# Clearing 896 unused words on GpSimd ahead of every four gathers of the second graph layer

## The reference, cut to what matters

```python
h = (x @ W).reshape(n, NHEAD, OUT_FEATS)            # 6250 nodes, 4 heads of 64
h_l, h_r = (a_l * h).sum(-1), (a_r * h).sum(-1)
e = h_l[row] + h_r[col]                              # 100000 edges
e = jnp.where(e > 0, e, ALPHA * e)
ex = jnp.exp(e - segment_max(e, row)[row])
denom = jax.ops.segment_sum(ex, row, num_segments=n)
att = ex / (denom[row] + 1e-16)
out = jax.ops.segment_sum(att[:, :, None] * h[col], row, num_segments=n)
```

## Time and profile before

| | us |
|---|---|
| three runs | 4160.5, 4170.12, 4170.46 |
| median | 4170.12 |
| profiled execution, its own time | 4167.99 |
| its span | 4166.3 |
| the block of the visits, POOL's first gather to DVE's last addition | 2048.7 to 3420.0 |

### The profile page before, as it was taken

How to read it: one execution, slowest core, us unless ns; L and a number is a source line. 1 busy time by engine, 2 the same in 40 slices (tenths; PEclk the granted TensorE clock), 3 DMA queues, 4 the chain that set the end, 5 groups by cost and what they waited for, 6 DMA issues and landing times. The chain is left out here.

```text
span 4166.3 us, 48622 instructions
## 1 busy us (share of the span) xinstructions
PE 2771.2 (67%) x12850; PEld 2189.0 (53%) x12850; DVE 2489.0 (60%) x5847; ACT 1566.9 (38%) x5077; POOL 2220.9 (53%) x2162
## 2 busy tenths in 40 slices
PE   5466776567677754824666676666667665699983
PEld 4233344355555543713555465555555545599972
DVE  5345998677777786434545555555555567544438
ACT  6663000067787831113422232233233223333334
POOL 0366777766666602555256666666666641265530
PEclk9678888788898965967867767677776675799985
DMA  5232333323333313632234444444444464122234
GB/s 146 86 88 83 89 87 89 88 85 90 90 93 91 95 57 91 152 76 71 78 89 114 109 114 113 109 115 109 113 113 112 111 112 150 62 72 70 71 96 143
DMA packets 220767, 408.50 MB, mean 98 GB/s; under 512 B 51598, under 2 KB 134545, under 8 KB 220371
## 3 DMA queue, kind: packets, MB, share of 16 engines
q0 software_dynamic: 102192, 279.12, 25.2%
q1 hardware_dynamic: 118308, 126.27, 10.2%
HBM read 342.96 MB, written 62.28 MB: 97 GB/s over the span
## 5 line engine op out<-in xcount | busy, mean ns | idle before, releaser
L534 POOL DMA_INDIRECT arena<-h_table,arena x1712 | 1751.6, 1023 | 1016.0 <-issue 482.5
L548 DVE TENSOR_TENSOR arena<-arena,ps 128x260 f32 (+1 forms) x1712 | 719.6, 420 | 905.0 <-remote 407.0
L2199 PE MATMUL ps<-arena 128*128 128x260 f32 x1760 | 667.1, 538 | 415.9 <-DVE arena L548 282.6
L2199 PEld LDWEIGHTS ps<-arena 128*128 128x128 f32 x1760 | 441.5, 268 | 591.3 <-issue 457.0
L1216 PE MATMUL ps<-arena 128*128 128x256 f32 x1664 | 556.7, 451 | 252.5 <-DVE arena L548 133.1
L1216 PEld LDWEIGHTS ps<-arena 128*128 128x128 f32 x1664 | 328.1, 222 | 410.2 <-issue 238.2
L717 ACT ACTIVATE arena<-arena 128x112 f16<-128x112 f16 x1568 | 446.5, 375 | 88.1 <-DVE arena L983 77.6
L2066 ACT ACTIVATE ps<-arena 128x32 f32<-128x32 f32 x110 | 22.1, 201 | 953.8 <-DVE arena L2122 784.6
L884 DVE TENSOR_SCALAR arena<-arena 128x128 f32<-128x128 f32 x832 | 290.4, 350 | 0.4
L2181 PEld LDWEIGHTS ps<-arena 128*128 128x128 f32 x1760 | 273.2, 236 | 16.6 <-issue 4.5
L2132 DVE TENSOR_TENSOR arena<-arena,ps 128x1024 f32<-128x1024 f32 x220 | 267.2, 1215 | 0.0
(11 more groups left out here) (520 smaller groups left out, 4289.0 us busy)
## 6 DMA issues: line engine op xcount, KB each, us to landing
arena<-visit_lanes SPq DMA_DIRECT2D x110, 256.0 KB
arena<-h_table,arena POOLq DMA_INDIRECT x1712
arena<-in_L_ffn_w SPq DMA_DIRECT2D x32, 512.0 KB, 7.4
xn_table<-arena SPq DMA_DIRECT2D x14, 896.0 KB, 4.0
slot_out<-arena SPq DMA_DIRECT2D x21, 512.0 KB
arena<-y_rows SPq DMA_DIRECT2D x12, 896.0 KB, 9.5
h_table<-arena SPq DMA_DIRECT2D x7, 924.0 KB
h_table<-arena SPq DMA_DIRECT2D x7, 896.0 KB, 4.2
```

The costliest lines, as they stand in the source:

```text
L534: pool.indirect_dma_start(slot[:, 0:width], None, table, bass.IndirectOffsetOnAxis(ap=idx, axis=0)).then_inc(done, 16)
L548: dve.tensor_tensor(to, to, bank(b, width), ALU.add).then_inc(gnn_add, 1)
L2199: pe.matmul(bank(sum_bank(g * U + u), ACC_W), hot[:, g % 3, u, :], rows[r][:, u, 0:ACC_W], start=True, stop=True).then_inc(gnn_ps, 1)
```

## The change

Ahead of every four gathers but the first four, behind the wait that stands there already, POOL fills `v_w` (128 partitions x 896 words of 32 bits) with zeros and waits for that to be done. There are 219 such turns: 880 / 4, less the first. Seven of them belong to groups 0 to 3, 212 to groups 4 to 109.

```diff
                         elif n % U == 0 and r:
                             pool.wait_ge(mx_ps, -(-r * SLOT_W // (B * D)))
                         pool.sem_inc(dma_turn, 1)
+                        if n:
+                            G.then(pool.memset(v_w, 0.0))
                     gather_row(pool, rows[r][:, u, :], ROW1, v_idx[:, n:n + 1], h1_table, rows_done[r])
```

## The result

| | before | after |
|---|---|---|
| median, us (runs, lowest to highest) | 4170.29 (4, 4160.5 to 4179.18) | 4119.94 (4, 4117.49 to 4127.34) |
| ratio | | 0.9878, 95% interval 0.9859 to 0.9896 |

The changed kernel is 1.2% **faster**, by some 50 us. The forecast was 95 us slower, 4265.

A forecast was written before the change was run, and what follows sets the result against it. No engine was full; POOL and its consumers were coupled, and the fills would make POOL the pacer. 307 us of turns less 194 of waiting and 14 of tail gave +99, so 4265 us; range 4190 to 4350.

The forecast's parts named there:

- What bounds the kernel: Long stretch of the block: no engine full, POOL and consumers coupled at 12.06 us a group, POOL able to do 10.18.
- The fill, 0.84 us: POOL's memset of 896 words, ahead of four gathers: 840 ns, estimated from fills of 1 and 128 words.
- The wait, 0.77 us in place of 0.30: POOL's gather behind the fill: starts 0.77 us after release, instead of the ordinary 0.30 us gap.
- the last of the signs: Named proof of being wrong, in the changed kernel's profile: the gather follows the memset at 0.3 us.
- The fill's start and signal, 0.10 + 0.04 us: On POOL each turn: 0.1 us for the fill to start behind the gather, 0.04 us for its signal.
- X = 1.45: POOL's added time per turn of four gathers, 1.45 us; ends 0.9 and 2.3.
- point of decision: X = 0.92 us a turn, where two turns use up POOL's spare 1.83 us a group.
- 194 - 14: Savings set against the fills: 194 us of POOL's true waiting in the long stretch, 14 us behind its last gather.
- The start at nothing: Groups 0 to 3: seven turns costing 10 us lie in 22 us of POOL idleness, so they add nothing.
- Contention with DVE: A fill meeting DVE's L2106 held at most 0.75 us, in perhaps 1 of 8 turns: 0.1 us on X.
- The memset fits into the idle time: Rival in the block: with X at 0.9, POOL's pauses free the consumers, 4150 us; chance faster 0.03, no change 0.05.
- The waits stay: Rival: POOL's full-ring waits stay and memsets come on top, 4475 us, or about 4370 with half recovered; chance 0.09.

The follow-up runs named there:

- double: The changed kernel with two fills of 896 words per turn, both waited for: 4314.22 us, ratio 1.0419 to the kernel before.
- event: The changed kernel with the wait for the fill on its own instruction, the increment of dma_turn, not on the gather: 4228.48 us, ratio 1.0197 to the kernel before.
- early: The changed kernel with the 896-word fills only in groups 0 to 3, seven of them: 4122.88 us, ratio 0.9960 to the kernel before.
- half: The changed kernel with the fill cut from 896 to 448 words: 4126.60 us, ratio 0.9959 to the kernel before.
- word: The changed kernel with a one-word fill and the wait for it on its own instruction: 4156.01 us, ratio 0.9962 to the kernel before.
- ring of three: The kernel before, no fill, with POOL at most three groups ahead of PE's count instead of four: 4135.29 us, ratio 0.9995.
- lumped: The changed kernel with two 896-word fills ahead of every eight gathers, none in the middle of a group: 4143.00 us, ratio 0.9934 to the kernel before.
- after, again: The changed kernel, unaltered, run once more on another chip: 4128.89 us, ratio 0.9892 to the kernel before.
- quarter: The changed kernel with a 224-word fill and the wait for it on its own instruction: 4142.64 us, ratio 0.9923 to the kernel before.
- after: The changed kernel in its first measurement, 896-word fills added to the kernel before: 4119.94 us, ratio 0.9878.
- three quarters: The changed kernel with 672 words filled in place of 896: 4103.19 us, ratio 0.9916 to the kernel before.
- late: The changed kernel with the fills only from group 4 on, none in groups 0 to 3: 4118.52 us, ratio 0.9943 to the kernel before.
- spread: The changed kernel with 168 words filled and waited for ahead of every gather, not 896 ahead of every four: 4141.25 us, ratio 1.0007 to the kernel before.

## Why the prediction was wrong, point by point

- **What bounds the kernel: right.** POOL had 1.83 us a group to spare, and with the fills it is the pacer and DVE waits for its rows.
- **The fill, 0.84 us: right.** 0.86 measured. The line through the small fills holds: 1 word 114 ns, 168 words 254, 224 words 305, 448 words 488, 672 words 678, 896 words 862 (medians of the fills in the traces), 0.84 ns a word. By the Trainium skill (Perfetto Trace Analysis, GPSIMD Engine Instruction), which advises to time GpSimd by the spacing of starts, I had an estimate of 0.98. The trace does not bear the 0.98 out: where two fills stand in a row (double), their starts are 0.92 us apart, of which some 0.87 is the recorded duration of the first; and here the recorded 0.86 and the 0.27 us behind it are together the spacing of 1.13 from the fill's start to the gather's. The 0.98 came from scaling up a spacing of 0.14 us between fills of which neither waited for the other, not from the duration.
- **The wait, 0.77 us in place of 0.30: wrong, and this is the step that failed.** 0.27 us was measured, which is the last of the signs that I had named for being wrong (a gather that follows the memset at 0.3 us). I took the price from two gathers that had been released by PE and did not ask which instruction carried the wait. There it is the increment ahead of the gather; in the change it is the gather. The event run put it on the increment and got my price (0.79) and nearly my time: 13.00 us a group against 13.08 forecast, ratio 1.0197 against my 4267 / 4168 = 1.024.
- **The fill's start and signal, 0.10 + 0.04 us: wrong.** The fill starts at the gather's end (0.1 us of idle time in all 211), and the signal is inside the 0.27.
- **So X = 1.45 was 0.83.** My own point of decision was 0.92, and I put a chance of 0.03 on the far side of it. With 0.83 the same sum gives 212 x 0.83 - 194 - 14 = -32 us. The start (below) adds -15, the gathers themselves got quicker (813.3 us for 823.9, -11), and the tail gave 6 us and not 14 (+8): -50 us, as measured.
- **The start at nothing: wrong.** I saw POOL idle for 22 us there and took the seven fills for free. They are better than free: early alone gives 0.40%. The earlier trace rows had the hint, PE busy for 16 of 22 us with POOL at rest; I didn't look at what DVE had waited for ahead of 2092.28.
- **Contention with DVE: right to leave small.** Four of the 219 fills overlap L2108 in the changed kernel's trace and none of them got longer (0.86 to 0.87 us); three of these L2108 were recorded with 1.57, 1.99 and 2.14 us in place of 0.75. With other sizes it is the fill that gets longer: in the half kernel 20 of 219 took over 0.9 us in place of 0.49. The Trainium skill (SBUF — State Buffer, Who interferes with whom) speaks of an exclusive lock for a whole instruction between DVE's two-port modes and GpSimd; that trace agrees in kind, L2108 at 2600.33 for 0.75 us and a fill of 1.00 us from 2600.48:

```profile
2600.33 0.75 DVE L2108 TENSOR_SCALAR arena<-arena 128x1024 f32<-128x1024 bf16 x1
2600.48 1.00 POOL L2049 MEMSET arena<- 128x448 f32 x1
```

- **The rivals.** "The memset fits into the idle time" is what happened, by its mechanism and its sign (4150 forecast for X = 0.9). "The waits stay" is refuted for POOL with this fill: no true wait of POOL is left. DVE's waits for counts do stay in part, and cost nothing there. POOL's stay where the fill is too short to make it the pacer (half and word: 11.8 to 11.9 us a group for an own pace of 11.2 to 11.4).

**What stays open.** Why the consumers follow at only 11.7 to 12.07 us a group while POOL gathers faster than that, though they need 7.5 us once it has stopped, and why PE's counts then come up to 11 us late. The runs speak against the lead (one step, ring of three) and against the length of a row of gathers alone (lumped). Being the faster side is not what brings these waits either: they are there with POOL as the pacer (174.3 us in "after, again", 230.0 in "quarter"). What the traces show in addition: of DVE's 40 waits of over 3 us for a count in the long stretch of the kernel before, 37 are for the first visit of a group, and in "after", "after, again" and "three quarters" all of them are (17, 51, 53). In the kernel before 36 of the 40 end when POOL has issued nothing for more than 1.2 us. For the wait of the earlier trace rows the trace has the four counts of the matmuls recorded at 2501.26 to 2503.25, and they come between 2512.16 and 2512.29. A rival that no run tests: right ahead of a group's first matmul PE loads the tile numbers of a group to come into its registers (`load_tiles`), which the profile does not record for PE; DVE's own load of such numbers takes 1.85 us each time, held or not. It would leave the waits in the mix unexplained, where PE loads no such numbers between its matmuls. A kernel that loads all tile numbers ahead of the block would tell. At the start, DVE's longest wait in the mix is 19.1 to 23.5 us in the kernels without a fill there (before, late, ring of three), 10.8 and 8.9 us in half and word, and at most 7.3 us in the others, down to 1.6 (event) and 2.4 (spread). By what means the gathers hold PE or its counts was not found.

## What to carry to other kernels

Ask of every wait which instruction carries it: on the gather itself it cost 0.27 us, on a small instruction ahead of it 0.79, and that alone decided the sign here. If an engine has spare time of s a turn, work out from which price of an edit it becomes the pacer, and when your price hangs on one uncertain term that could move it across that point, give the other side a real chance. An engine's idle time in front of a full ring is not only cover: filling it just up to the crossing shortened the stretch, the tail and the start, while overfilling it (double, event) cost every microsecond.

## What the runs showed of the hardware that I had not expected

- A fill on POOL begins within the record's resolution at the end of the indirect gather ahead of it, while a gather behind a gather starts 0.30 us after its end. A fill of w words (128 partitions) takes 0.11 + 0.00084 w us, from 1 to 896 words.
- At the start of the block POOL's unbroken gathers and PE's slow progress go together. In the changed kernel the 14 matmuls of one mix step (28 records, each matmul has two) stand in one row:

```profile
2073.33 3.39 PE L2171 MATMUL ps<-arena 128*128 128x128 f32 x28 [0.15 <-DVE arena L2143]
```

In the kernel before, L2169, while POOL gathers without a break, records of such matmuls come singly, 2.1 us apart in these two rows, and PE waits ahead of them for nothing that the profile shows:

```profile
2083.82 0.37 PE L2169 MATMUL ps<-arena 128*128 128x128 f32 x1 [0.84 <-issue]
...
2085.92 0.37 PE L2169 MATMUL ps<-arena 128*128 128x128 f32 x1 [1.73 <-issue]
```

None of these records is missing: both traces have 196 of them, 7 steps of 28. Ahead of L2169 the "issue" waits of PE are 22.6 us in 24, ahead of L2171 4.3 us in 2. DVE's wait of 23.45 us stands behind them. At the start, a break of 1.1 us at every fourth gather, or of 0.53 at each, makes it go (early, spread); what the gathers hold there was not found.
